# Reordered loads, ScalarE zero-fills, later gate and weight folds and query blocks over three queues in a transformer layer's opening

## The reference, cut to what matters

```python
mod = (silu(c) @ wmod).reshape(4, 6, 1, 128)           # c: 4 x 128
sa, ca, ga, sb, cb, gb = mod[:, 0], ..., mod[:, 5]
ga = (2 * (ga >= 0) - 1) * maximum(abs(ga), 0.25)       # gb the same way
h = layernorm(x) * (1 + ca) + sa                        # x: 4 batches x 512 tokens x 128
x = x + ga * attention(h)      # 16 heads of 8, rotary, causal softmax, output projection
h = layernorm(x) * (1 + cb) + sb
x = x + gb * experts(h)        # 8 slices a token, 16 experts, top 2 by softmax of logits
```

## Time and profile before

| | us |
|---|---|
| median of 3 runs | 442.27 (441.61 to 442.72) |
| the profiled execution, its own time | 441.48 |
| its span | 439.7 |
| PE busy | 353.3 (80%) |
| VectorE busy | 298.0 (68%) |
| ScalarE busy | 242.2 (55%) |
| GpSimd busy | 111.2 (25%) |

### The profile page before, as it was taken

The page is one execution under the profiler, slowest core; times in us unless marked ns, Lnnn a source line. Parts: engine busy times, 40 slices in busy tenths (PEclk is TensorE's granted clock), DMA queues, the critical chain, the costliest instruction groups (busy, mean ns, idle before and its releaser), DMA issues.

```text
span 439.7 us, 7235 instructions
## 1 busy us (share of the span) xinstructions
PE 353.3 (80%) x2652; PEld 164.3 (37%) x2684; DVE 298.0 (68%) x596; ACT 242.2 (55%) x291; POOL 111.2 (25%) x151
## 2 busy tenths in 40 slices
PE   0555386888867978999879969998879798879995
PEld 0532142445534444443444434433545323123122
DVE  7479994575878797777576877786549456943342
ACT  1102023344224786887534868875457887858970
POOL 8334720000524020443250204433130023122000
PEclk9996666999989999999998999999999999989999
DMA  8102410000220182554001715551105155704550
GB/s 291 25 1 68 79 46 24 3 5 0 50 29 2 39 106 71 137 143 110 2 25 31 95 51 141 135 133 22 28 0 73 36 144 160 117 2 121 151 135 24
DMA packets 26847, 31.43 MB, mean 71 GB/s; under 512 B 6454, under 2 KB 17718, under 8 KB 26678
## 3 DMA queue, kind: packets, MB, share of 16 engines
q1 hardware_dynamic: 23740, 28.84, 28.3%
q0 software_dynamic: 3072, 2.13, 2.8%
HBM read 3.47 MB, written 1.05 MB: 10 GB/s over the span
## 4 chain that ended last, share of the span: by engine, by line
PE 53%; DVE 19%; ACT 10%; issue 7%; SPq 4%; DMA 4%; POOL 1%; ACTq 0%; DVEq 0%; POOLq 0%
PE acc L1125 17%; PE big L1125 17%; PE misc L1125 17%; ACT ring L657 7%; DVE mx L897 6%; DVE xn L838 3%; DMA q_dense<-nm 2%; PE misc L1144 2%; SPq L425 2%; SPq L446 1%; ACT qk_turned L665 1%; SPq L380 1%; DVE stats L813 1%; DMA q_dense<-qk 1%; ACT L690 1%
## 5 line engine op out<-in xcount | busy, mean ns | idle before, releaser
L657 ACT ACTIVATE ring<-big 128x1024 f32<-128x1024 f32 (+1 forms) x224 | 197.3, 932 | 124.5 <-PE big L1125 123.2
L897 DVE TENSOR_REDUCE mx<-misc 128x1 f32<-128x320 f32 (+7 forms) x154 | 86.9, 589 | 36.0 <-PE misc L1125 34.6
L1125 PE MATMUL acc<-ring,cb 128*32 128x512 f32 x512 | 68.8, 612 | 5.4 <-ACT ring L657 4.4
L1125 PE MATMUL big<-tstack,w1s 128*128 128x512 bf16 x177 | 52.4, 381 | 10.0 <-ACT ring L657 7.1
L1125 PE MATMUL big<-q_dense,k_block 128*128 128x448 bf16 (+7 forms) x249 | 53.4, 320 | 5.2 <-DMA q_dense<-nm 3.1
L1125 PE MATMUL misc<-k_dense,q_block 128*128 128x384 bf16 (+7 forms) x171 | 43.6, 318 | 6.4 <-DVE mx L897 5.9
L1020 DVE SCALAR_TENSOR_TENSOR gm<-acc,cb,gm 128x512 f32<-128x512 f32 x40 | 29.9, 747 | 27.3 <-DMA gm<-wT 14.5
L1125 PEld LDWEIGHTS big<-q_dense,k_block 128*128 128x128 bf16 x256 | 30.8, 148 | 31.1 <-ACT ring L657 14.3
L1125 PEld LDWEIGHTS misc<-k_dense,q_block 128*128 128x128 bf16 x174 | 21.3, 149 | 52.1 <-DVE mx L897 37.0
L1125 PE MATMUL acc<-ring,vals 128*32 128x64 f32 (+7 forms) x512 | 40.1, 421 | 0.4
L1125 PE MATMUL big<-earlier_query,identb 128*128 128x64 bf16 (+2 forms) x176 | 37.0, 210 | 2.5 <-DMA q_dense<-nm 1.8
(11 more groups left out here) (160 smaller groups left out, 486.2 us busy)
## 6 DMA issues: line engine op xcount, KB each, us to landing
gm<-wT SPq DMA_DIRECT2D x64, 256.0 KB
tstack<-tp SPq DMA_DIRECT2D x18, 128.0 KB, 5.1
k_block<-qk_turned POOLq DMA_DIRECT2D x48, 32.0 KB, 3.6
q_dense<-qk SPq DMA_DIRECT2D x24, 64.0 KB
ca<-in_pack_a SPq DMA_DIRECT2D x1, 1155.0 KB, 5.4
k_dense<-qk SPq DMA_DIRECT2D x18, 64.0 KB
...
```

The source lines that it names most:

```text
L657: act.activation(dst, src, func, scale=scale).then_inc(s["ring_read"], 1)
L897: dve.tensor_reduce(mx[:, g, k:k + n, blk], src, AX.X, ALU.max).then_inc(s["misc_read"], 1)
L1125: return pe.matmul(dst, lhsT, rhs, start=start, stop=stop)
```

## The change

The packs: c and wmod move from pack_a to a pack_c of their own. SyncE issues x of batch 0, pack_c, pack_a, x of batch 1, w1, pack_b, x of batches 2 and 3, with semaphores of their own for the first ones.

Zero-fills: GpSimd first writes a column of zeros (`nought`) and fills q_block; ScalarE fills k_dense, vals, q_dense and k_block by copying `nought` broadcast along the row, and, after its share of the query blocks, tstack and the upper half of gm. VectorE fills nothing.

Order on VectorE: statistics of batch 0, silu, normalise, modulation, modulate. On PE: modulation, first norm, projection, values, then the gate matmuls. ScalarE copies the raw gates to SBUF beside their absolute values. The gate folds follow the eighth and ninth of the 17 points of the first softmax, and the four instructions of the weight cut follow the 11th to 14th (each point's maxima stand ahead of the insert).

Query blocks of batch 0: four of SyncE's eight go to ScalarE's queue (`FROM_SCALAR = 4`). GpSimd's `stack_q(1)` moves ahead of `fold_out(0)`.

```diff
+FOLD_AT, CUT_AT = len(WOVEN) // 2 - 1, [len(WOVEN) // 2 + 2 + k for k in range(4)]
...
+        graw = [gm[:, k, :].rearrange("p (b d) -> p b d", b=NB) for k in (0, 7)]
...
-            sp.dma_start(ca[:, :], pack_a).then_inc(s["a_loaded"], 16)
             xv = x.rearrange("b (t p) d -> p b t d", p=P)
             sp.dma_start(xs[:, 0], xv[:, 0]).then_inc(s["x0_loaded"], 16)
+            sp.dma_start(cc[:, :], pack_c).then_inc(s["c_loaded"], 16)
+            sp.dma_start(ca[:, :], pack_a).then_inc(s["a_loaded"], 16)
+            sp.dma_start(xs[:, 1], xv[:, 1]).then_inc(s["x1_loaded"], 16)
             sp.dma_start(w1f, w1_rows).then_inc(s["w1_loaded"], 16)
             sp.dma_start(cb[:, :], pack_b).then_inc(s["b_loaded"], 16)
-            for b in range(1, NB):
+            for b in range(2, NB):
                 sp.dma_start(xs[:, b], xv[:, b]).then_inc(s["x_loaded"], 16)
             for n in ("k_dense_stacked", "q_block1_stacked", "q_dense_stacked", "shift_stacked0", "shift_stacked1", "t_stacked", "stored"):
                 sp.sem_inc(s[n], CREDIT[n])
-            sp.wait_ge(s["zeroed"], 1)
+            sp.wait_ge(s["k_block_cleared"], 1)
...
-                for c, a in Q_BLOCKS[1]:
+                for c, a in Q_BLOCKS[1][0 if b else FROM_SCALAR:]:
...
-            sp.wait_ge(s["cleared"], 2)
+            sp.wait_ge(s["cleared"], 1)
             stack_k(0)
-            sp.wait_ge(s["zeroed"], 2)
+            sp.wait_ge(s["zeroed"], 1)
             stack_q_block(0)
+            sp.wait_ge(s["cleared"], 3)
             stack_q(0)
-            sp.wait_ge(s["zeroed"], 4)
+            sp.wait_ge(s["spare_cleared"], 2)
             stack_k(1)
...
+            pool.memset(nought[:, :], 0.0).then_inc(s["nought_ready"], 1)
+            pool.memset(q_block[:].rearrange("r p a t -> r (p a t)").bitcast(F32), 0.0).then_inc(s["zeroed"], 1)
...
-            pool.memset(k_block[:].rearrange("r p a t -> r (p a t)").bitcast(F32), 0.0).then_inc(s["zeroed"], 1)
-            pool.memset(q_block[:].rearrange("r p a t -> r (p a t)").bitcast(F32), 0.0).then_inc(s["zeroed"], 1)
-            pool.wait_ge(s["zeroed"], 2)
+            pool.wait_ge(s["zeroed"], 1)
...
-            pool.memset(tstack[:].rearrange("r p t -> r (p t)").bitcast(F32), 0.0).then_inc(s["zeroed"], 1)
-            pool.memset(gm[:, GMS // 2:GMS, :].rearrange("p k t -> p (k t)"), 0.0).then_inc(s["zeroed"], 1)
             rsqrt(1, 0)
-            pool.wait_ge(s["zeroed"], 4)
             stack_q(0)
             pool.wait_ge(s["ones_loaded"], 16)
             stack_k(0)
             k_blocks(K_BLOCKS)
+            pool.wait_ge(s["spare_cleared"], 2)
+            stack_q(1)
             pool.wait_ge(s["b_loaded"], 16)
-            pool.wait_ge(s["x_loaded"], 16 * (NB - 1))
             pool.wait_ge(s["x0_loaded"], 16)
+            pool.wait_ge(s["x1_loaded"], 16)
+            pool.wait_ge(s["x_loaded"], 16 * (NB - 2))
             pool.wait_ge(s["gates_filled"], 2)
             fold_out(0)
-            stack_q(1)
...
-            act.wait_ge(s["a_loaded"], 16)
-            act.activation(sil[:, 0, :], A["cT"], ACT.Exp, scale=-1.0).then_inc(s["exp_ready"], 1)
-            act.wait_ge(s["gates_filled"], 1)
-            for k in range(2):
-                act.activation(gabs[k], big[:, 1 + k, :].rearrange("p (b d) -> p b d", b=NB), ACT.Abs)\
-                   .then_inc(s["abs_ready"], 1)
+
+            def clear(t, ready):
+
+                act.copy(t, nought[:, 0:1].to_broadcast([P, t.shape[1]])).then_inc(s[ready], 1)
+
+            act.wait_ge(s["nought_ready"], 1)
+            clear(k_dense[:].rearrange("r p t -> r (p t)").bitcast(F32), "cleared")
+            clear(vals[:].rearrange("q p s w -> q (p s w)"), "cleared")
+            act.wait_ge(s["c_loaded"], 16)
+            act.activation(sil[:, 0, :], C["cT"], ACT.Exp, scale=-1.0).then_inc(s["exp_ready"], 1)
+            clear(q_dense[:].rearrange("r p t -> r (p t)").bitcast(F32), "cleared")
+            clear(k_block[:].rearrange("r p a t -> r (p a t)").bitcast(F32), "k_block_cleared")
+
+            def take_gates():
+
+                act.wait_ge(s["gates_filled"], 1)
+                for k in range(2):
+                    raw = big[:, 1 + k, :].rearrange("p (b d) -> p b d", b=NB)
+                    act.activation(gabs[k], raw, ACT.Abs).then_inc(s["abs_ready"], 1)
+                    act.copy(graw[k], raw).then_inc(s["abs_ready"], 1)
+
+            def stack_q_block():
+
+                act.wait_ge(s["zeroed"], 1)
+                act.wait_ge(s["qk_turned"], 3)
+                for c, a in Q_BLOCKS[1][:FROM_SCALAR]:
+                    block_diagonal(act, q_block, c, a, PARTS_L[c], 0, "q_block1")
...
+            stack_q_block()
+            clear(tstack[:].rearrange("r p t -> r (p t)").bitcast(F32), "spare_cleared")
+            clear(gm[:, GMS // 2:GMS, :].rearrange("p k t -> p (k t)"), "spare_cleared")
+            take_gates()
...
+            def modulation():
+
+                dve.wait_ge(s["mod_ready"], 1)
+                link(dve.tensor_copy(mod[:].rearrange("p k b -> p (k b)"), big[:, 0, 0:6 * NB]))
+                for k in (1, 4):
+                    link(dve.tensor_scalar(mod[:, k, :], mod[:, k, :], 1.0, None, ALU.add))
+
+            def silu():
+
+                dve.wait_ge(s["exp_ready"], 1)
+                link(dve.tensor_scalar(sil[:, 1, :], sil[:, 0, :], 1.0, None, ALU.add))
+                link(dve.reciprocal(sil[:, 0, :], sil[:, 1, :]))
+                dve.tensor_tensor(sil[:, 2, :], sil[:, 0, :], C["cT"], ALU.mult).then_inc(s["sil_ready"], 1)
+                dve.wait_ge(s["sil_ready"], 1)
+                dve.tensor_copy(silb, sil[:, 2, :].unsqueeze(2).to_broadcast([P, NB, P])).then_inc(s["sil_ready"], 1)
+
+            def ones_for_sums():
+
+                dve.wait_ge(s["cleared"], 2)
+                for a in range(2):
+                    link(dve.memset(vals[BLK * a:BLK * a + BLK, :, :, (HS + 1) * a + HS:(HS + 1) * a + HS + 1], 1.0))
+
+            def fold_gates(k):
+
+                dve.wait_ge(s["abs_ready"], 2 * k + 2)
+                link(dve.tensor_scalar(graw[k], graw[k], 0.0, 2.0, ALU.is_ge, ALU.mult))
+                link(dve.tensor_scalar(gabs[k], gabs[k], 0.25, None, ALU.max))
+                link(dve.scalar_tensor_tensor(out=gate[:, k, :, :], in0=graw[k], scalar=-1.0, in1=gabs[k],
+                                              op0=ALU.add, op1=ALU.mult))
+
+            def cut_weights(part):
                 dve.wait_ge(s["b_loaded"], 16)
                 dve.wait_ge(s["w1_loaded"], 16)
                 less1, less2 = B["keep"][:, 0:1], B["keep"][:, 1:2]
+                if part == 0:
+                    link(dve.tensor_copy(w1p, w1f))
+                elif part == 1:
+                    link(dve.scalar_tensor_tensor(out=w1f, in0=w1p, scalar=less1, in1=w1f, op0=ALU.mult, op1=ALU.add))
+                elif part == 2:
+                    link(dve.tensor_copy(w1p, w1f))
+                else:
+                    link(dve.scalar_tensor_tensor(out=w1s[:, :], in0=w1p, scalar=less2, in1=w1f, op0=ALU.mult, op1=ALU.add))
...
-            here = ("first", 0)
+            here, ahead = ("first", 0), ("second", 0)
             dve.wait_ge(s["x0_loaded"], 16)
             norm_link = links("ln_link", LN_LINKS, 0)
             statistics(xs[:, 0], 0, 0, 0, norm_link)
+            silu()
             normalise(xs[:, 0], 0, 0, norm_link)
+            modulation()
+            pick_modulation(0, 0)
+            dve.wait_ge(s["a_loaded"], 16)
             modulate(0, hT, here, "xT", 0)
             wait_read(dve, here, "xT")
-            dve.wait_ge(s["x_loaded"], 16 * (NB - 1))
+            dve.wait_ge(s["x1_loaded"], 16)
             norm_link = links("ln_link", LN_LINKS, 1)
             statistics(xs[:, 1], 1, 1, 0, norm_link)
             rotate(here, 0)
             cut_rotated(0)
             normalise(xs[:, 1], 1, 0, norm_link)
+            ones_for_sums()
             values(here, 0)
-            ahead = ("second", 0)
             modulate(0, hT, ahead, "xT", 1)
-            fold_gates()
             rotate(ahead, 1)
-            cut_weights()
             maxima(here, 0, ALONE[:4])
             cut_rotated(1)
             maxima(here, 0, ALONE[4:])
-            for at, uses in WOVEN.items():
+            for k, (at, uses) in enumerate(WOVEN.items()):
                 if at[0] == "first":
                     maxima(here, 0, uses)
                 else:
                     maxima(ahead, 1, uses)
+                if k in (FOLD_AT, FOLD_AT + 1):
+                    fold_gates(k - FOLD_AT)
+                if k == FOLD_AT + 1:
+                    dve.sem_inc(s["gates_filled"], 1)
+                if k in CUT_AT:
+                    cut_weights(CUT_AT.index(k))
+            dve.wait_ge(s["x_loaded"], 16 * (NB - 2))
...
-            pe.wait_ge(s["a_loaded"], 16)
+            pe.wait_ge(s["c_loaded"], 16)
             pe.wait_ge(s["sil_ready"], 1)
```

(20 more changed lines are left out.)

55 lines of the change are left out of this document (17 added, 38 removed).

## The result

The changed kernel takes 432.56 us (median of 4 runs, 429.73 to 437.61) against 442.22 us (441.61 to 442.72): the ratio is 0.9755, 95% interval 0.972 to 0.9791. It is faster by 9.7 us, where 14.8 was forecast. In a later comparison the same kernel took 432.53 us (430.71 to 438.47, 6 runs), ratio 0.9782 (0.9752 to 0.9812). The medians take in every execution; the ratios leave out the slow ones, over 1.5% above the fastest of their kernel (here 437.61 and 438.47). The profiled execution of after took 429.73 us, that of before 441.48: 11.75 us apart. So there are two questions: where 3.1 us of the forecast went inside the profiled execution, and why the median gained 2.1 us less than that execution.

A forecast was written before the change was run, and what follows sets the result against it. The opening's single chain and first softmax were taken as the bound on what the change could win. 15.5 (head) + 0 (covered work) + 2.7 (queues) less 3.4 (inserts) is 14.8: 442.3 to 427.5 us, range 422 to 434.

The forecast's parts named there:

- The head: Opening up to hT's first write: hT at 11.1 to 11.3 us instead of 26.79, 15.5 us less.
- Both arms: Two chains up to hT: GpSimd's fill, power and normalisation, to 9.75 us; ScalarE's fills, exp and modulation matmuls, to 9.7.
- that of the strided copy: ScalarE's fills in the opening at the slow price, about 4.1 us per 2048 columns: 431.8; 0.12 shared with second table load.
- Covered work: Gate matmuls, spare fills and other work moved under idle time in the opening: 0 us.
- Three queues: Query blocks of batch 0 over three queues: SyncE's dense rows go out and the cut comes sooner, 2.7 us less.
- The cut then waits for the dense rows: Second batch's cut on VectorE: follows the dense rows' last issue by 5.1 us, so comes 2.7 us sooner.
- The rival at 0.13: Query block stage: issues exclude each other, or landings, not issues, set the dense rows; 430.2 us; chance 0.13.
- the exclusive descriptor generator: ScalarE's four block issues queue with SyncE's four, 1.3 us each, so three queues give nothing: 430.2 us; within the 0.13.
- Inserts: Gate folds and weight cuts between maxima of the first softmax: 3.4 us more, bounds 0 to 7.4.
- the wait forecast at 1.85 us: First softmax, behind fold two: PE's third unit waits 1.85 us more for VectorE's maxima.
- The rival took the low level through the whole softmax: VectorE's inserts idle PE, keeping its clock low through the first softmax: up to 18 us, 445.5; chance 0.02.

The follow-up runs named there:

- a2_sp_eight: The changed kernel with all eight query blocks back on SyncE, none on ScalarE; 430.23 us, ratio 0.972 to the kernel before.
- e1: The changed kernel with GpSimd's key blocks held until the dense rows landed and SyncE's dense rows waiting for the query blocks; 430.74 us, ratio 0.9726 to before.
- a4: The changed kernel with all eight query blocks on SyncE and GpSimd's key blocks held until the dense rows landed; 430.09 us, ratio 0.9725 to before.

## Why the prediction was right or wrong

**The head: right.** 15.5 us were forecast, 15.7 came (hT 11.11; forecast 11.1 to 11.3). Both arms held: the power ended at 7.93 (forecast 7.95), xn at 9.74 (9.75), and exp ended at 5.97 (6.2). The fills went at ScalarE's row price (1.90 and 3.60 us, forecast 1.87 and 3.6), not that of the strided copy. Only the modulation was earlier than thought, 9.42 instead of 9.7, with no effect.

**Covered work: right.** The gates' matmuls (2.05 us now, not 3.8), the spare fills and the folding of x cost nothing that the trace shows. The distance from hT to the turned copies went from 11.64 (26.79 to 38.43) to 11.72 us (11.11 to 22.83).

**Three queues: wrong.** The step that failed is "The cut then waits for the dense rows", with its last issue to cut in 5.1 us, and "The new last issue ends at 45.2: the cut at 50.3, 2.7 us sooner." It took the landing as a fixed distance from the issue. The issues did end sooner, but the landings moved the other way: SyncE's four issues took 2.71 us, its dense rows were out at 29.7 (forecast 29.7 on the new clock), and the cut came at 38.14 instead of 34.8. Relative to the head's gain that is 0.8 us lost, not 2.7 won: a term wrong by 3.5 us and in sign. And it was no longer the dense rows that the cut waited for, but the query blocks. The rival at 0.13 ("the landings, not the issues, set the dense rows") had the mechanism, but gave it zero as its worst; the price below zero was left out. The prediction put PE's start on them 3.5 us behind the last block's issue (42 to 45.5), and it was 8.8. The first four maxima, forecast to end by 32.9 (48.4 less 15.5), could not begin until PE had them, at 35.37. A row of before, on PE's timeline, could have warned and was not read:

```profile
48.54 0.26 PE L1125 MATMUL misc<-later_key,identb 128*128 128x64 bf16 x1 [5.15 <-DMA q_block<-qk_turned]
```

SyncE's last block was issued by 43.9; PE waited 5.15 us and had it at 48.5, 4.6 us after that. So already before, PE stood still for a landing, and the issue was half of it at most. The same distance is 3.3 us in a2_sp_eight (28.27 to 31.61), 8.8 in after (26.6 to 35.37), 2.6 in e1 and 1.9 in a4: it is no constant but what the traffic beside it makes of it.

The issues themselves: SyncE's stayed at 0.68 us each (forecast 0.67) and GpSimd's at 0.64. ScalarE's four took 3.68 us: the first 1.51, the other three 0.72 each on average, and so in every run that issues from ScalarE. SyncE's and ScalarE's overlap, so the exclusive descriptor generator that the prediction weighed, of the Trainium skill's "Perfetto Trace Analysis", section "DMA Instruction — HWDGE (DVE, Sync)", does not show as a serialisation to 1.3 us each between SyncE and ScalarE. Issues that exclude each other for all of their length are ruled out; what the 1.51 us of ScalarE's first are, no run shows.

**Inserts: right in place and size.** 3.4 us forecast, 3.3 measured (43.17 to 46.47), 3.0 of it in PE's waits for maxima; the wait forecast at 1.85 us is the one of 1.81. Without the inserts the length is back at 43.30, with them in the gap at 43.44. Not seen in the forecast: a place where they cost nothing existed on the same engine.

**The clock.** The rival took the low level through the whole softmax, 18 us, at 0.02; that did not come. A smaller form did, in some executions: up to 1.1 us in the softmax and 2.5 in the later round compared above. The forecast subtracted a profiled difference from a median, which is good only to the 2 us and more by which executions of one kernel differ.

**The sum.** In the profiled executions: 15.7 less 0.8 less 3.3 is 11.6, against 11.75 measured. In the medians 9.7; the 2.1 between are that the profiled execution of after was a fast one, with a high granted clock. That the clock is all of it is argued from the executions above, not shown. The forecast of 14.8 was 5.1 too high: 3.5 from the queues, 2.1 from the difference between median and profiled execution, and 0.5 the other way in small ones. That 432.6 still lies between 422 and 434 is partly luck: one of the three large terms had the wrong sign, and the range was wide enough for it because it allowed for slow fills, which did not come.
